# Cross-attention of a Perceiver layer: four of seventeen value steps in three f32r passes, head pairs written out, sums spread one step earlier

## The chip, the cores and the metric

One core of a Trainium2 chip runs the whole kernel in one launch. The time is that of the device in microseconds (us), as the median of several executions. The engines are named as in the profile: PE (TensorE), with its weight loads apart as PEld, DVE (VectorE), ACT (ScalarE), POOL (GpSimd) and SP (SyncE, which only issues DMAs here).

## What is computed

A layer on 256 tokens of 1024 features, in float32: a cross-attention of the normalised tokens over 4096 context rows and the tokens themselves (32 heads, 4 key heads, width 128), then a decayed linear attention, then a small mixture of low-rank experts. The change is in the first part:

```python
q = (latents @ Wq).reshape(b, q_len, N_KV_HEADS, N_GROUPS, HEAD_DIM)
k = (hidden_states @ Wk).reshape(b, kv_len, N_KV_HEADS, HEAD_DIM)
v = (hidden_states @ Wv).reshape(b, kv_len, N_KV_HEADS, HEAD_DIM)
scores = jnp.einsum('bqhgd,bkhd->bhgqk', q, k) * scale
attn = jax.nn.softmax(scores.astype(jnp.float32), axis=-1).astype(q.dtype)
out = jnp.einsum('bhgqk,bkhd->bqhgd', attn, v)
return out.reshape(b, q_len, N_HEADS * HEAD_DIM) @ Wo
```

## The kernel before

Most matrix products are made of three passes in float32r, a rounded float32: each operand is split into a high part (rounded) and a low part (the rest), and `three_pass` (L111) adds high x high, high x low and low x high. One product is not: probabilities by values is a plain float32 matmul (L903), which the trace records as two instructions a tile.

Stages, one after another: `project_keys_values` (stage 1, 0 to 380 us) reads the context in 8 chunks of 512 rows and makes keys (split, kept in DRAM as kT_hi, kT_lo) and values (plain, v_scratch), while POOL splits the query weights. `cross_attention` (380 to 1370 us) runs the 16 pairs of heads. `project_out` (the wo stage) multiplies with Wo, adds x and normalises; `linear_attention`, a second `project_out` and `lora_mixture` follow.

A pair has 17 steps j of 256 key rows, 512 query columns wide (two heads by 256 tokens). The work of two pairs n and n+1 is interleaved, and each engine's order is written out by hand in its slot function; semaphores tie them. In step j:

- PE (`pe_slot`, L925): values of pair n, step j (2 tiles, L903); scores of pair n+1, step j+2 (2 tiles, three passes, L870). After step 5 the predecessor's sums are spread over the partitions (`pe_sums`, L907); after step 15 comes the transpose of the peaks; at the end the maximum is spread and the query projection of pair n+3 is made (48 passes). Two score buffers: scores j+2 wait for ACT's row copy of step j.
- DVE (`dve_slot`, L810): subtracts the maximum from the rows of pair n, step j+1 (`dve_shift`, L790), takes the running peak of pair n+1, step j (`dve_peak`, L765 to L778), and in steps 6 to 9 a quarter each of the reciprocal of the sums (`dve_inverse`, L798).
- ACT (`act_slot`, L661): exp of pair n, step j+1, into one of three buffers `probs` (L649); copy of the score rows of pair n+1, step j (L631); in step 1 also the high part of the predecessor's sums (`act_sum`, L653).
- POOL (`pool_slot`, L726): adds the probabilities of step j to `sums` (L702, L705); in step 3 the low part of the predecessor's sum (`pool_sum_low`, L717), in step 11 the predecessor's output product (L724), at the end the sum of the two halves (L712).
- SP (`sync_slot`, L584): weights of pair n+3, keys of the next key head in every fourth pair, values in the next, by four pieces of columns.

`slots` (L551) runs pair 0, then a hardware loop of three rounds with four pairs each (1 to 12), then pairs 13 to 15 written out. The last pair has no successor: DVE takes four of the sixteen adds there, and PE makes the spread of the sums from plain float32 tiles (`pe_sums_last`, L915).

Of the kernel before, what the change touches and what calls it, by code (L numbers as in the profile page):

```python
# [87 lines left out]
class Shared:  # L88
# [3 lines left out]
    def __init__(self, a):  # L92
# [7 lines left out]
        self.v_stored = a.sem("v_stored")  # L100
        self.first_in = a.sem("first_in")
# [102 lines left out]
def project_keys_values(nc, x, ctxT, wk, wv, wq, x_sb, hT_hi, hT_lo, ident, ones, k_drams, v_dram, wq_drams, shared):  # L204
# [5 lines left out]
    with ExitStack() as ctx:  # L210
        a = Alloc(nc, ctx, "kv_")
        w_raw = a.sb("w_raw", [P, KT, KVH * D])
# [9 lines left out]
        v_out = carve(shared.stage, 0, KVH, CCHUNK // P, D)  # L222
        k_ps = a.ps("k_ps", [P, KVH, BANK])
# [44 lines left out]

        @block.sync
        def _(sp):  # L270
# [12 lines left out]
            with sp.Fori(0, NCHUNK - 3) as c:  # L283
                sp.wait_ge(c_lo_ready, c + 1)
                load(sp, c + 2)
                store(sp, c, VT)
            sp.wait_ge(c_lo_ready, NCHUNK - 2)
            load(sp, NCHUNK - 1)
            store(sp, NCHUNK - 3, VT)
            store(sp, NCHUNK - 2, VT)  # L290
# [8 lines left out]
            store(sp, NCHUNK - 1, VT)  # L299
            store(sp, NCHUNK, QT)  # L300
# [60 lines left out]

        def copy_low_keys(dve, c, n):
# [12 lines left out]
        def _(dve):  # L375
# [92 lines left out]
KEEP = 3  # L468
# [12 lines left out]
def cross_attention(nc, wq_drams, k_drams, v_dram, hT_hi, hT_lo, ident, ones, oT_dram, shared, proj, last_pair):  # L481
# [9 lines left out]
    with ExitStack() as ctx:  # L491
        a = Alloc(nc, ctx, "xa_")
        kT_hi, kT_lo = shared.r
        v = a.sb("v", [P, KV])
        more_rows = a.sb("rows", [P, J - ENDS[0], 2, W])
        rows = [carve(shared.f, 2 * W * j, 2, W) for j in range(ENDS[0])] + [more_rows[:, j] for j in range(J - ENDS[0])]
        probs = [carve(shared.stage, 2 * W * i, 2, W) for i in range(2)] + [a.sb("probs", [P, 2, W])[:, :, :]]
# [24 lines left out]
        v_in = [a.sem(f"v_in{i}") for i in range(len(ENDS))]  # L522
        q_done = a.sem("q_done")
# [25 lines left out]
        def slots(eng, slot):  # L549
# [4 lines left out]
            with eng.Fori(0, KVH - 1) as g:  # L554
# [1262 lines left out]
```

## Time and profile before

| | |
|---|---|
| time, median of 3 runs | 2001.52 us (2000.62 to 2008.04) |
| the profiled execution's own time | 1999.74 us |
| its span | 1997.9 us |
| PE busy | 1960.9 us (98%), granted clock 0.996 of full speed |
| PEld, DVE, ACT, POOL busy | 76%, 62%, 48%, 42% |
| values, plain float32 (L903) | 1088 instructions, 512 us |
| DMA | 283.85 MB, mean 142 GB/s |

A busy matmul is one whose modelled end has not come, so 98% does not say that PE is at its peak; what a tile costs is read from the distance of starts. The chain at the page's end covers only the last 15 us. For the cross-attention the timelines of single engines tell the order, and a releaser in brackets tells what an engine waited for.

### The profile page before, as it was taken

What the parts mean: (1) busy time and instruction counts of PE and PEld (TensorE: products, weight loads), DVE (VectorE), ACT (ScalarE), POOL (GpSimd) and SP (SyncE); (2) the same over time, 40 slices, a digit from 0 to 9 for tenths busy, and PEclk for the clock granted to TensorE, in tenths of its full rate; (3) what the DMA queues carried; (4) which work ended last, traced back from release to release, by engine and by line L of the source; (5) the groups of instructions that cost most, each with busy time, mean ns of one, the idle gap of its engine ahead of it and who ended that gap; (6) DMA issues with size and microseconds to landing.
All of it is one profiled execution on the core that took longest, in us unless ns stands there. A gap on an engine that the chain in (4) does not pass through costs nothing. (4 is left out here: it accounts for less than half of the span.)

```text
span 1997.9 us, 26905 instructions
## 1 busy us (share of the span) xinstructions
PE 1960.9 (98%) x9725; PEld 1516.6 (76%) x9725; DVE 1233.5 (62%) x1294; ACT 952.7 (48%) x1015; POOL 839.3 (42%) x410
## 2 busy tenths in 40 slices
PE   9999999999999999999999999998999999999998
PEld 7888888866666666666666666545899999999876
DVE  4432221266777777877677877787756666666556
ACT  3211110155665565665665665654635444555442
POOL 2545441026776666766767766783000000000200
PEclk9999999999999999999999999999999999999999
DMA  8788875420032210321112210014735544445462
GB/s 306 301 305 318 327 271 190 173 99 25 24 111 90 72 49 15 111 97 56 49 52 92 79 61 1 6 58 180 282 138 189 185 177 175 178 182 189 139 232 99
DMA packets 72224, 283.85 MB, mean 142 GB/s; under 512 B 6400, under 2 KB 24320, under 8 KB 56512
## 3 DMA queue, kind: packets, MB, share of 16 engines
q1 hardware_dynamic: 65216, 232.31, 32.3%
q0 software_dynamic: 6912, 50.33, 6.6%
q8 instruction: 51, 0.84, 0.2%
q14 instruction: 45, 0.37, 0.1%
HBM read 212.89 MB, written 69.73 MB: 141 GB/s over the span
## 5 line engine op out<-in xcount | busy, mean ns | idle before, releaser
L705 POOL TENSOR_TENSOR xa_sums<-xa_sums,stage 128x1024 f32<-128x1024 f32 x150 | 362.7, 2418 | 39.3 <-ACT stage L649 33.1
L903 PE MATMUL xa_o_ps<-stage,xa_v 128*128 128x512 f32 x768 | 361.8, 594 | 4.5 <-ACT stage L649 4.5
L769 DVE TENSOR_TENSOR xa_peak<-xa_s_ps,xa_peak 128x1024 f32<-128x1024 f32 x224 | 273.0, 1219 | 71.4 <-PE xa_s_ps L115 70.8
L113 PE MATMUL xa_s_ps<-xa_qT_hi,split 128*128 128x512 f32 x544 | 304.7, 560 | 6.2 <-issue 3.5
L631 ACT ACTIVATE xa_rows<-xa_s_ps 128x1024 f32<-128x1024 f32 x208 | 213.6, 1027 | 102.0 <-DVE xa_peak L769 69.9
L790 DVE TENSOR_TENSOR xa_rows<-xa_rows,xa_r_ps 128x1024 f32<-128x1024 f32 x208 | 248.1, 1195 | 0.0
L903 PEld LDWEIGHTS xa_o_ps<-stage,xa_v 128*128 128x128 f32 x768 | 144.2, 190 | 116.9 <-issue 99.2
L705 POOL TENSOR_TENSOR xa_sums<-xa_sums,xa_probs 128x1024 f32<-128x1024 f32 x75 | 178.9, 2386 | 124.7 <-ACT xa_probs L649 122.1
L115 PE MATMUL xa_s_ps<-xa_qT_hi,split 128*128 128x512 f32 x544 | 214.4, 394 | 0.0
L114 PE MATMUL xa_s_ps<-xa_qT_lo,split 128*128 128x512 f32 x544 | 212.6, 391 | 0.0
L649 ACT ACTIVATE stage<-xa_rows 128x1024 f32<-128x1024 f32 x144 | 152.5, 1060 | 66.5 <-DVE xa_rows L790 61.6
L1418 DVE TENSOR_TENSOR pair_lo<-pair_raw,pair_hi 128x4096 fp32r<-128x4096 f32 x30 | 132.8, 4426 | 81.4 <-ACT pair_hi L1355 81.4
L1345 POOL TENSOR_TENSOR square_sum<-square_sum,la_squares 128x512 f32<-128x512 f32 x16 | 20.8, 1301 | 385.7 <-ACT la_squares L1385 385.7
L113 PEld LDWEIGHTS xa_s_ps<-xa_qT_hi,split 128*128 128x128 f32 x544 | 102.4, 188 | 78.3 <-issue 41.5
L903 PE MATMUL xa_o_ps<-xa_probs,xa_v 128*128 128x512 f32 x320 | 150.5, 593 | 1.7 <-ACT xa_probs L649 1.7
L114 PEld LDWEIGHTS xa_s_ps<-xa_qT_lo,split 128*128 128x128 f32 x544 | 102.7, 189 | 65.1 <-issue 52.0
L113 PE MATMUL la_qk_ps<-hT_hi,pair_hi 128*128 128x256 f32 x512 | 145.6, 284 | 0.3 <-PEq L1018 0.3
L115 PE MATMUL la_qk_ps<-hT_hi,pair_lo 128*128 128x256 f32 x512 | 144.8, 283 | 0.0
L114 PE MATMUL la_qk_ps<-hT_lo,pair_hi 128*128 128x256 f32 x512 | 144.7, 283 | 0.0
L307 ACT ACTIVATE kv_k_hi<-kv_k_ps 128x512 fp32r<-128x512 f32 (+1 forms) x36 | 20.4, 573 | 209.0 <-DMA kT_lo_scratch<-kv_k_lo 105.4
L115 PEld LDWEIGHTS xa_s_ps<-xa_qT_hi,split 128*128 128x128 f32 x544 | 102.0, 188 | 23.6
L366 DVE TENSOR_TENSOR kv_k_lo<-kv_k_ps,kv_k_hi 128x512 fp32r<-128x512 f32 (+1 forms) x36 | 23.6, 659 | 138.4 <-ACT kv_k_hi L307 138.4
(308 smaller groups left out, 4629.7 us busy)
## 6 DMA issues: line engine op xcount, KB each, us to landing
pair_raw<-in_w_qk SPq DMA_DIRECT2D x15, 2048.0 KB, 7.7
pair_raw<-in_w_gv SPq DMA_DIRECT2D x15, 2048.0 KB, 7.7
kv_w_raw<-in_wq POOLq DMA_DIRECT2D x16, 1024.0 KB, 8.3
wq_hi_scratch<-x_hT_hi POOLq DMA_DIRECT2D x16, 1024.0 KB, 4.5
wq_lo_scratch<-x_hT_lo POOLq DMA_DIRECT2D x16, 1024.0 KB, 5.3
full<-in_wo SPq DMA_DIRECT2D x16, 1024.0 KB, 5.1
pair_raw<-in_w_out SPq DMA_DIRECT2D x16, 1024.0 KB, 5.0
xa_w_hi<-wq_hi_scratch SPq DMA_DIRECT2D x15, 1024.0 KB, 4.8
```

The costliest lines, as they stand in the source:

```text
L113: pe.matmul(out, w_hi, m_hi, start=first, stop=False)
L114: pe.matmul(out, w_hi, m_lo, start=False, stop=False)
L115: return pe.matmul(out, w_lo, m_hi, start=False, stop=last)
L366: dve.tensor_tensor(k_lo[:, g % 2, 0:n], k_ps[:, g, 0:n], f32(k_hi[:, g % 2, 0:n]), ALU.subtract).then_inc(k_copied, 1)
L631: act.activation(rows[j], s_ps[:, 2 * b:2 * b + 2, :], ACT.Copy).then_inc(row_ready, 1)
L649: act.activation(probs[j % KEEP], rows[j], ACT.Exp, scale=SCALE).then_inc(exp_done, 1)
L705: pool.tensor_tensor(sums[:, :, :], sums[:, :, :], probs[j % KEEP], ALU.add).then_inc(added, 1)
L769: dve.tensor_tensor(peak[:, :, :], s_ps[:, 2 * b:2 * b + 2, :], peak[:, :, :], ALU.max).then_inc(peak_done, 1)
L790: dve.tensor_tensor(rows[j], rows[j], r_ps[:, :].unsqueeze(1).to_broadcast([P, 2, W]), ALU.subtract).then_inc(shifted, 1)
L903: last = pe.matmul(o_ps[:, :], v[:, at], probs[j % KEEP][:, t, :], start=j == 0 and t == 0, stop=j == J - 1 and t == 1)
L1345: pool.tensor_tensor(square_sum[:, :, :], square_sum[:, :, :], squares[:, :, :], ALU.add).then_inc(sq_added, 1)
L1418: dve.tensor_tensor(w_lo[part][:, :, :], raw[part][:, :, :], f32(w_hi[part][:, :, :]), ALU.subtract).then_inc(w_lo_ready[part], 1)
```

## The change

- In steps 2, 6, 10 and 14 of each pair the value product is made in three f32r passes. Stage 1 splits the values of those tiles (`split_values` on DVE) and stores the low parts in a tensor of their own; a pair loads v, v_hi and v_lo. ACT makes the exp of such a step twice, once into `probs` and once rounded into `probs_hi`; POOL subtracts (`pool_low`) into `probs_lo`. There is one tile each of probs_hi and probs_lo. The row sums still take the unrounded `probs`.
- `probs` has four buffers (KEEP) in place of three, and shift and exp run two steps ahead (AHEAD) in place of one.
- The loop over key heads is written out in every engine's program.
- The sum's high part moves from ACT's step 1 to step 0, its low part from POOL's step 3 to step 1, the spread on PE from step 5 to step 4, the reciprocals from steps 6 to 9 to 5 to 8.
- To make room, `inverse` shares the tile of `sum_row`, x is a tile of stage 1 and loaded a second time in the wo stage, and the identity and the ones are rounded once, in the first block, and no longer in the attention's.

```diff
 LAST_BY_POOL = tuple(j for j in range(1, J) if j not in LAST_BY_VECTOR)
-KEEP = 3
+SPLIT_STEPS = (2, 6, 10, 14)
+SPLIT = len(SPLIT_STEPS)
+KEEP = 4
+AHEAD = 2
...
-            with eng.Fori(0, KVH - 1) as g:
+            for g in range(KVH - 1):
                 for u in (1, 2, 3, 0):
                     slot(eng, 4 * g + (u or 4), u, g if u else g + 1)
...
         def act_exp(act, n, j, first=False, last=False):
...
             act.activation(probs[j % KEEP], rows[j], ACT.Exp, scale=SCALE).then_inc(exp_done, 1)
+            if j in SPLIT_STEPS:
+                i = SPLIT_STEPS.index(j)
+                if i > 0:
+                    act.wait_ge(pv_done, J * n + SPLIT_STEPS[i - 1] + 1)
+                elif not first:
+                    act.wait_ge(pv_done, J * (n - 1) + SPLIT_STEPS[-1] + 1)
+                act.activation(probs_hi[:, :, :], rows[j], ACT.Exp, scale=SCALE).then_inc(probs_hi_ready, 1)
...
-                if has_prev and j == 1:
+                if has_prev and j == 0:
                     act_sum(act, n - 1)
...
+        def pool_low(pool, n, j):
+
+            pool.wait_ge(exp_done, J * n + j + 1)
+            pool.wait_ge(probs_hi_ready, SPLIT * n + SPLIT_STEPS.index(j) + 1)
+            pool.tensor_tensor(probs_lo[:, :, :], probs[j % KEEP], f32(probs_hi[:, :, :]), ALU.subtract).then_inc(low_by_pool, 1)
...
-                if has_prev and j == 3:
+                if j in SPLIT_STEPS:
+                    pool_low(pool, n, j)
+                if has_prev and j == 1:
                     pool_sum_low(pool, n - 1)
...
-                if has_prev and 6 <= j < 10:
-                    dve_inverse(dve, n - 1, j - 6)
+                if has_prev and 5 <= j < 9:
+                    dve_inverse(dve, n - 1, j - 5)
...
+            if j in SPLIT_STEPS:
+                pe.wait_ge(low_by_pool, SPLIT * n + SPLIT_STEPS.index(j) + 1)
+                for t in range(2):
+                    at = slice(split_columns(j).start + t * P, split_columns(j).start + (t + 1) * P)
+                    last = three_pass(pe, o_ps[:, :], v_hi[:, at], v_lo[:, at], probs_hi[:, t, :], probs_lo[:, t, :],
+                                      False, False)
+                last.then_inc(pv_done, 1)
+                return
...
-                if has_prev and j == 5:
+                if has_prev and j == 4:
                     pe_sums(pe, n - 1)
```

In stage 1 and in the wo stage:

```diff
+        def split_values(dve, c, t, i):
+
+            dve.wait_ge(v_ready, VT * c + t + 1)
+            dve.tensor_copy(v_out[:, :, t, :].bitcast(F32R), v_ps[:, t, :].rearrange("p (g d) -> p g d", d=D)).then_inc(v_rounded, 1)
+            dve.wait_ge(v_rounded, 2 * i + t + 1)
...
+                    last = dve.tensor_tensor(tile, v_ps[:, t, g0 * D:g1 * D].rearrange("p (g d) -> p g d", d=D),
+                                             v_out[:, g0:g1, t, :], ALU.subtract).then_inc(low_copied, 1)
...
+            if i == 3:
+                sp.dma_start(x_sb[:, :, :], x).then_inc(x_in, 16)
             weights.load_half(sp, i // 2, i % 2)
```

How the hand-written orders move shows at two places. The first is POOL's program from the end of pair 0 into pair 1. `xa_sum_row` is the predecessor's sum, `xa_sum_hi` its high part from ACT, `xa_exp_done` and the like are semaphores. Before:

```order
L702 TENSOR_TENSOR xa_sums<-stage 128x1024 [waits xa_sum_made,xa_exp_done]
...
L705 TENSOR_TENSOR xa_sums<-xa_sums,xa_probs 128x1024 [waits xa_added]
...
L705 TENSOR_TENSOR xa_sums<-xa_sums,stage 128x1024 [waits xa_added]
L717 TENSOR_TENSOR xa_sum_lo<-xa_sum_row,xa_sum_hi 128x512 [waits xa_sum_made,xa_sum_hi_ready]
```

and now:

```order
L814 TENSOR_TENSOR xa_sum_row<-xa_sums 128x512 [waits xa_added]
L798 TENSOR_TENSOR xa_sums<-stage 128x1024 [waits xa_sum_made,xa_exp_done]
L819 TENSOR_TENSOR xa_sum_lo<-xa_sum_row,xa_sum_hi 128x512 [waits xa_sum_made,xa_sum_hi_ready]
L801 TENSOR_TENSOR xa_sums<-xa_sums,xa_probs0 128x1024 [waits xa_added,xa_exp_done]
L807 TENSOR_TENSOR xa_probs_lo<-xa_probs0,xa_probs_hi 128x1024 [waits xa_probs_hi_ready,xa_exp_done]
L801 TENSOR_TENSOR xa_sums<-xa_sums,xa_probs1 128x1024 [waits xa_added,xa_exp_done]
```

The sum's low part stands behind the first add (step 1) in place of the third (step 3), ahead of the first probs_lo. The second place is ACT's program at a split step (step 10 of pair 0, whose exp is issued in step 8), now:

```order
L718 ACTIVATE xa_rows<-xa_s_ps 128x1024 [waits xa_exp_done,xa_peak_done]
L736 ACTIVATE xa_probs0<-xa_rows 128x1024 [waits xa_added,xa_pv_done,xa_shifted]
L743 ACTIVATE xa_probs_hi<-xa_rows 128x1024 [waits xa_pv_done]
L718 ACTIVATE xa_rows<-xa_s_ps 128x1024 [waits xa_exp_done,xa_peak_done]
L736 ACTIVATE xa_probs1<-xa_rows 128x1024 [waits xa_added,xa_pv_done,xa_shifted]
```

Two exps stand between two row copies there, where one stood before.

## Rows read from the trace of the kernel before

**Rows 1.** Timeline of ACT, 660 to 800 us: start, us, engine, line, operation, [idle <- releaser]
```profile
668.30 0.60 ACT L659 ACTIVATE xa_o_raw<-xa_o_ps 128x512 f32<-128x512 f32 x1 [1.48 <-PE xa_o_ps L903]
...
728.20 0.60 ACT L659 ACTIVATE xa_o_raw<-xa_o_ps 128x512 f32<-128x512 f32 x1 [1.48 <-PE xa_o_ps L903]
...
790.13 0.60 ACT L659 ACTIVATE xa_o_raw<-xa_o_ps 128x512 f32<-128x512 f32 x1 [1.48 <-PE xa_o_ps L903]
```

**Rows 2.** Timeline of PE where the loop turns round
```profile
736.13 0.49 PE L113 MATMUL xa_s_ps<-xa_qT_hi,split 128*128 128x512 f32 x1 [1.79 <-issue]
```

**Rows 3.** Timeline of PE, pair 13 (x4: two f32 tiles)
```profile
1220.06 1.88 PE L903 MATMUL xa_o_ps<-stage,xa_v 128*128 128x512 f32 x4
1221.38 0.79 PE L113 MATMUL xa_s_ps<-xa_qT_hi,split 128*128 128x512 f32 x1
...
1223.17 1.88 PE L903 MATMUL xa_o_ps<-stage,xa_v 128*128 128x512 f32 x4
...
1238.67 0.40 PE L912 MATMUL xa_t_ps<-xa_sum_hi,xa_ones_r 128*128 128x512 f32 x1
...
1239.13 1.88 PE L903 MATMUL xa_o_ps<-stage,xa_v 128*128 128x512 f32 x4
```

**Rows 4.** Timeline of POOL, pair 13
```profile
1216.02 2.41 POOL L702 TENSOR_TENSOR xa_sums<-stage 128x1024 f32<-128x1024 f32 x1 [6.37 <-ACT stage L649]
...
1224.99 2.40 POOL L705 TENSOR_TENSOR xa_sums<-xa_sums,stage 128x1024 f32<-128x1024 f32 x1 [0.17 <-ACT stage L649]
1227.34 1.30 POOL L717 TENSOR_TENSOR xa_sum_lo<-xa_sum_row,xa_sum_hi 128x512 fp32r<-128x512 f32 x1
1228.59 2.39 POOL L705 TENSOR_TENSOR xa_sums<-xa_sums,stage 128x1024 f32<-128x1024 f32 x1
1231.12 2.39 POOL L705 TENSOR_TENSOR xa_sums<-xa_sums,xa_probs 128x1024 f32<-128x1024 f32 x1
```

**Rows 5.** Timeline of ACT, pair 13
```profile
1213.83 2.11 ACT L649 ACTIVATE stage<-full 128x1024 f32<-128x1024 f32 x2 [1.90 <-DVE full L790]
1220.16 1.02 ACT L631 ACTIVATE full<-xa_s_ps 128x1024 f32<-128x1024 f32 x1 [4.22 <-DVE xa_peak L765]
...
1222.42 1.03 ACT L631 ACTIVATE full<-xa_s_ps 128x1024 f32<-128x1024 f32 x1
1223.35 0.62 ACT L653 ACTIVATE xa_sum_hi<-xa_sum_row 128x512 fp32r<-128x512 f32 x1
...
1244.47 1.06 ACT L649 ACTIVATE stage<-xa_rows 128x1024 f32<-128x1024 f32 x1 [0.92 <-DVE xa_rows L790]
1245.60 1.02 ACT L631 ACTIVATE xa_rows<-xa_s_ps 128x1024 f32<-128x1024 f32 x1
```

**Rows 6.** Timeline of DVE, pair 13
```profile
1218.90 1.22 DVE L765 COPY xa_peak<-xa_s_ps 128x1024 f32<-128x1024 f32 x1 [4.05 <-PE xa_s_ps L115]
...
1239.33 0.96 DVE L798 RECIPROCAL xa_inverse<-xa_t_ps 128x128 f32<-128x128 f32 x1 [2.34 <-PE xa_t_ps L913]
1240.20 1.16 DVE L790 TENSOR_TENSOR xa_rows<-xa_rows,xa_r_ps 128x1024 f32<-128x1024 f32 x1
...
1242.41 0.95 DVE L798 RECIPROCAL xa_inverse<-xa_t_ps 128x128 f32<-128x128 f32 x1
```

**Rows 7.** Timeline of PE, start of pair 14
```profile
1276.24 0.50 PE L113 MATMUL xa_s_ps<-xa_qT_hi,split 128*128 128x512 f32 x1 [0.18 <-ACT full L631]
```

**Rows 8.** Timeline of POOL, pair 15, first and last add
```profile
1329.69 2.37 POOL L735 TENSOR_TENSOR xa_sums<-stage 128x1024 f32<-128x1024 f32 x1 [5.38 <-ACT stage L649]
...
1363.19 3.14 POOL L738 TENSOR_TENSOR xa_sums<-xa_sums,stage 128x1024 f32<-128x1024 f32 x1
```

**Rows 9.** Timeline of POOL, rounding of the constants
```profile
382.44 0.28 POOL L748 CAST xa_ident_r<-ident 128x128 fp32r<-128x128 f32 x1 [74.92 <-POOLq L210]
```

**Rows 10.** Busy time by stretch: us, PE, PEld, DVE, ACT, POOL, clock, DMA share, GB/s
```profile
150.00:200.00 50.00, 50.00 (x222) 41.41 (x221) 12.39 (x10) 6.63 (x6) 25.24 (x16) 1.00 0.84 317
1375.00:1450.00 75.00, 75.00 (x332) 62.10 (x331) 54.49 (x55) 42.97 (x50) 0.00 (x0) 1.00 0.80 292
```

More of the change, by code:

```diff
@@ L282, in _ @@
             sp.dma_start(x_sb[:, :, :], x).then_inc(x_in, 16)
[L283 to L286, printed above, removed]
+            sp.wait_ge(c_lo_ready, 1)
+            load(sp, 2)
+            store(sp, 0, VT)
+            with sp.Fori(0, (NCHUNK - 4) // 2) as i:
+                for par in range(2):
+                    c = 2 * i + 1 + par
+                    sp.wait_ge(c_lo_ready, c + 1)
+                    load(sp, c + 2)
+                    store(sp, c, VT)
+                    if par == 0:
+                        store_low(sp, c, i)
             sp.wait_ge(c_lo_ready, NCHUNK - 2)
@@ L478, in starts_piece, with plain_columns, split_columns, value_runs @@
     return j == 0 or j in ENDS
-def cross_attention(nc, wq_drams, k_drams, v_dram, hT_hi, hT_lo, ident, ones, oT_dram, shared, proj, last_pair):
+def plain_columns(j0, j1):
+    back = sum(s < j0 for s in SPLIT_STEPS)
+    return slice(2 * P * (j0 - back), 2 * P * (j1 - back))
+def split_columns(j):
+    i = SPLIT_STEPS.index(j)
+    return slice(2 * P * i, 2 * P * (i + 1))
+def value_runs(i):
+    runs, start = [], ENDS[i - 1] if i else 0
+    for j in range(start, ENDS[i]):
+        if j in SPLIT_STEPS:
+            if start < j:
+                runs.append((start, j))
+            runs.append((j, j + 1))
+            start = j + 1
+    if start < ENDS[i]:
+        runs.append((start, ENDS[i]))
+    return runs
+def cross_attention(nc, wq_drams, k_drams, v_dram, low_dram, hT_hi, hT_lo, ident, ident_r, ones_r, oT_dram, shared, proj, last_pair):
     with ExitStack() as ctx:
@@ L677, in act_slot @@
                 act_output(act, n, not has_prev)
-                act_exp(act, n + 1, 0)
+                for j in range(AHEAD):
+                    act_exp(act, n + 1, j, last=last and u == 2)
         @block.scalar
@@ L686, in _ @@
                     act_query(act, 1, 1)
-            act_exp(act, 0, 0, True)
+            for j in range(AHEAD):
+                act_exp(act, 0, j, True)
             slots(act, act_slot)
@@ L839, in _ @@
             dve_max(dve, 0, True)
-            dve_shift(dve, 0, 0)
+            for j in range(AHEAD):
+                dve_shift(dve, 0, j)
             slots(dve, dve_slot)
@@ L921, in pe_sums_last @@
             for i, part in enumerate(pieces):
-                last = pe.matmul(t_ps[:, :], ones[:, :], part, start=i == 0, stop=i == len(pieces) - 1)
+                last = pe.matmul(t_ps[:, :], f32(ones_r[:, :]), part, start=i == 0, stop=i == len(pieces) - 1)
             last.then_inc(sum_spread, 1)
```

124 lines of the change are left out of this document (87 added, 37 removed).

## The prediction, made before the changed kernel ran

> **What bounds the kernel now.** I read the page first: PE 98% busy, POOL 42%, and a chain that names only the last microseconds. So the views that matter are those of one stage. The cross-attention (430 to 1370 us) runs as 16 nearly equal head pairs; [rows 1] gives the moments at which ACT copies a pair's output: 59.90 us from one pair to the next, and 61.93 where the loop turns round, with a hole of 1.79 us in PE's stream [rows 2]. Elsewhere PE issues without a gap inside a pair, so the pair's length is PE's, and whatever PE newly waits for lands in the time.
>
> [rows 3] is PE in pair 13, which is straight-line code already, as all pairs will be. I call V0 = 1220.06 the start of value step 0. Scores of the next pair start at V0 + 1.31, and V1 is at V0 + 3.11: a step is 3.10 us. One f32r pass is 0.23 us (1238.67 to 1239.13 are two), so a step's six score passes take 1.38 and its two f32 tiles 1.72.
>
> [rows 4] is POOL. An add of the row sums runs 2.39 us; a dependent add follows after 2.53 (1228.59 to 1231.12), an independent instruction after 2.35 (1224.99 to 1227.34), and behind the half-size subtraction the next starts after 1.25. [rows 5] is ACT: an exp and its successor are 1.13 apart, a score-row copy and the next 0.93; POOL starts 0.08 after ACT's end. [rows 6] is DVE: it idles 4.05 us before the first peak copy, and in the four steps with a reciprocal its cycle is 3.08 us (1239.33 to 1242.41), the shift 0.87 behind the reciprocal. That is PE's step almost exactly: in these steps PE has no lead.
>
> **Part 1, the gain on PE.** 4 of 17 steps a pair go from 1.72 us of f32 to six f32r passes, 6 x 0.23 = 1.38: 0.34 less a step, 1.36 a pair. The last pair is not PE's (below), so 15 x 1.36 = 20.4 us is what is offered. Bounds: 0.31 to 0.38 a step, as the passes next to f32 work are slower or not. The Trainium skill, "FP8 and Floating Point Precision", section "TensorE Precision Notes", has true FP32 as four passes through the array; three in place of four would give back a quarter of 1.72, 0.43 a step, and the offered gain would be 25.8, the sum below 5.4 less. I take the row, since a pass with its weight load measures 0.23, not 1.72/8 = 0.215.
>
> **Part 2, the loop.** The loop over key heads turns round twice, and the pair there is 61.93 - 59.90 = 2.03 longer. Written out, both go: -4.1. The entry and the exit of the loop cost nothing that the periods show.
>
> **Part 3, POOL gets 4 subtractions a pair and an earlier wait.** Each split step's values wait for probs_lo, which POOL makes behind its add of the same step. Total work is no problem: 16 adds, 4 subtractions and three half-size ones are some 53 us of 60. The order is. POOL's program has, in a pair with a predecessor: add 1, then the low part of the predecessor's sum, then add 2, then probs_lo of step 2. The sum's low part waits for its high part, which ACT makes behind the row copy of the next pair's step 0; that copy starts at V0 + 0.10 [rows 5], because it needs the peak copy and this the scores. So, with V0 = 0: ACT sum_hi at 0.10 + 0.93 = 1.03, end 1.65; POOL sum_lo at 1.73 (it idles from the end of add 1, -1.63, to here), add 2 at 2.98, probs_lo at 5.33, end 7.73. PE wants it at 3.11 + 3.10 = 6.21 and gets it at 7.78: **a stall of 1.57 us**. Before, the same wait stood behind add 3 and cost nothing.
>
> Behind this POOL runs on: a block of four steps is 3 x 2.53 + 2 x 2.35 = 12.29 for POOL and 3 x 3.10 + 2.76 = 12.06 for PE. probs_lo of step 6 ends at 20.0, wanted at 20.3; of step 10 at 32.3; of step 14, with the output product (1.25) in between, at 45.7.
>
> **Part 4, ACT and DVE in the reciprocal steps.** The sums are spread after step 4 now, one step earlier for PE and DVE alike, V5 = 17.20. From there DVE's chain runs by the cycle of [rows 6]: shift 9 at V5 + 0.20 + 3.08 + 0.87 = 4.15, and ACT's exp 1.19 behind its start (1244.47 against 1243.28), the row copy 1.13 later, 1.02 long, then PE's scores after 0.06: V5 + 7.55. PE, one cheaper step in hand (step 6), wants them at 3.10 + 2.76 + 1.31 = 7.17. The next is worse: step 10's second exp (probs_hi, 1.13) stands ahead of row copy 8, so the scores start at 7.22 + 1.19 + 1.13 + 1.13 + 1.02 + 0.06 = 11.75 where PE without stalls is there at 10.27: **1.48 us lost**. What PE saved in step 6 is thus given back, and the exp on top. V14 comes out at 45.9, just behind POOL's 45.7, so that step 14 costs nothing more; if Part 4 were nil, POOL would hold PE at 45.7 anyway. The pair is longer by 1.57 + 1.48 - 1.36 = **+1.7 us**. From V16 to the next V0 nothing changes: exps of the next pair need POOL's add 16, at about 48.2, in time.
>
> The sum over pairs. Pair 0 has no predecessor, hence neither wait: -1.4. Pairs 1 to 13: 13 x 1.7 = +22.1. Pair 14 follows without a query projection between; ACT has exp 2 and its second copy (2 x 1.13) before row copy 0, on which PE already waits there [rows 7]: 1.7 + 2.3 = +4.0. Pair 15 has no next one, and POOL sets its end: 36.6 us from its first add to its last [rows 8], of which 12 adds at 2.53 and two products at 1.25 are 32.9. Four more instructions of 2.35 are 9.4; if they filled all the slack of 3.7 it would be +5.7, if new waits (for sum_hi, for the single probs_hi tile, free only after PE's split step) arise, up to +10. I take +8, nearer the upper end because each subtraction there sits between an exp and a PE step that frees the next.
>
> **Part 5, the rest.** The constants are now rounded in the first block, before anything else may start: two casts of 0.28 [rows 9], +0.6. Stage 1's extra copies and subtractions on DVE (4 chunks, 2 tiles each, some 0.7 us apiece) and 2 MB of stores on SP's queue lie beside a PE that has not one idle slice [rows 10] and a value bank that is needed a chunk later; cost 0, and if DMA at 0.84 of its share should choke, about 3 us. The value loads go from 4 to more, smaller transfers a group, wanted a pair later: 0. x is loaded a second time (1 MB) in the output projection, ahead of the last quarter weights; at 292 GB/s [rows 10] that is 3.4 us of DMA with 0.2 of the share free: 0 taken, 3 as the bound.
>
> Sum: 0.6 - 1.4 + 22.1 + 4.0 + 8.0 - 4.1 = **+29.2 us** on the profiled execution's own 1999.74, so 2028.9. The median of the runs shown is 1.8 above it: **2031 us**, slower by 1.5%.
>
> **The rivals.**
> *It does what it is written for* (10%). PE is the bound and stays it; the waits of Parts 3 and 4 are absorbed. For it: POOL has 42% on the page and 53 of 60 us now. Against it: PE has no slack in a pair, and the wait for sum_hi has no earlier work behind it that could hide. Then -15 x 1.36 - 4.1 + 8 + 0.6 = -16: 1985.
> *Only ACT's chain bites, POOL is in time at step 2* (8%), say because the high part of the sum comes earlier than I have it. A pair is then +1.48 - 1.36 = +0.1, and pair 14 +2.4: 13 x 0.1 + 2.4 + 8 - 1.4 - 4.1 + 0.6 = +7: 2006 to 2010, no change or just slower.
> *Only POOL bites* (inside my forecast): a pair is +1.4 by the 45.7 above, 2027.
> *More is queued than I see* (7%): POOL stretches when DVE works in SBUF alone, the x load holds up the projection, PE's clock falls in the new pauses. 15 x 1 us more and 3 for x: 2045 to 2050. The decision between same and slower is at one place, the start of probs_lo of step 2: if it started before V0 + 3.7 no pair would stall there.
>
> **How the numbers follow.** Forecast with its bounds 75%: 2015 (pairs at 1.0, the last at 5.7) to 2040. The range that leaves out no more than 2 in 10 takes in the upper part of the ACT-only case: 2010 to 2042. About 0.5% (10 us) is what a measurement of this kernel can tell from no change. Slower by more than that: the forecast and the bad case, 0.82, and a little of ACT-only, 0.83. Within it: 0.07. Faster: 0.10.
>
> **What would show it.** Right: pair period about 61.5 us without a longer one at the loop's old ends; in POOL's waits an entry of the sum's low part on ACT's sum_hi of some 3.4 us, 14 times; PE waiting 1.6 us on POOL's probs_lo at step 2, and on ACT's row copies about 1.5 us a pair at steps 7 and 8; the last pair 8 us longer. Wrong: a period under 59, or PE waiting nowhere inside a pair; a period over 63 would say that a queue is longer than I have it.

## The result and the profile after

The changed kernel takes **2034.74 us**, median of 4 runs (2032.27 to 2036.05), the kernel before on the same chip 2002.07 us (2000.62 to 2008.04). The ratio is 1.0156, with a 95% interval of 1.0141 to 1.0172: slower by 1.6%, 3.7 us above the forecast of 2031 and inside its range. The profiled execution took 2034.6 us. Its page begins:

```profile
span 2032.8 us, 26010 instructions
## 1 busy us (share of the span) xinstructions
PE 1958.4 (96%) x9853; PEld 1540.3 (76%) x9853; DVE 1266.1 (62%) x1306; ACT 1007.7 (50%) x1079; POOL 990.5 (49%) x474
```

PE is still busy for 96%, and POOL for 49% only. By these shares nothing but PE could be the bound, and they mislead here. What answers to [rows 1], ACT's copy of a pair's output, in the timeline of ACT after the change:

```profile
672.05 0.60 ACT L753 ACTIVATE xa_o_raw<-xa_o_ps 128x512 f32<-128x512 f32 x1 [1.41 <-PE xa_o_ps L1016]
733.47 0.60 ACT L753 ACTIVATE xa_o_raw<-xa_o_ps 128x512 f32<-128x512 f32 x1 [1.41 <-PE xa_o_ps L1016]
794.86 0.60 ACT L753 ACTIVATE xa_o_raw<-xa_o_ps 128x512 f32<-128x512 f32 x1 [1.41 <-PE xa_o_ps L1016]
```

61.42 and 61.39 us apart; from pair 0 to pair 13 (487.91 to 1285.96) the mean is 61.39, and no pair is longer where the loop turned round. Where PE stopped inside pair 13 (V0 = 1233.32), all its gaps from V0 to V14 in the timeline of PE, and V8 and V9 around the second:

```profile
1241.07 0.50 PE L114 MATMUL xa_o_ps<-xa_probs_hi,xa_v_hi 128*128 128x512 f32 x1 [1.38 <-POOL xa_probs_lo L807]
...
1259.67 1.88 PE L1016 MATMUL xa_o_ps<-stage,xa_v 128*128 128x512 f32 x4
...
1261.98 0.50 PE L114 MATMUL xa_s_ps<-xa_qT_hi,split 128*128 128x512 f32 x1 [0.44 <-ACT xa_rows L718]
...
1263.47 1.88 PE L1016 MATMUL xa_o_ps<-stage,xa_v 128*128 128x512 f32 x4
...
1279.02 0.50 PE L114 MATMUL xa_o_ps<-xa_probs_hi,xa_v_hi 128*128 128x512 f32 x1 [0.23 <-POOL xa_probs_lo L807]
```

V2 starts at V0 + 7.75, the scores of tile 10 at V5 + 11.38, V14 at V0 + 45.70. A bracket counts from the modelled end of the matmul before and is shorter than what the step loses. The distance of starts tells the loss: V1 to V2 is 4.64 us in place of 3.10 (1.54 lost), V8 to V9 3.80 in place of 3.11 (0.69), V13 to V14 3.49 in place of 3.10 (0.39).

POOL in the same pair, against [rows 4]:

```profile
1235.04 1.30 POOL L819 TENSOR_TENSOR xa_sum_lo<-xa_sum_row,xa_sum_hi 128x512 fp32r<-128x512 f32 x1 [3.35 <-ACT xa_sum_hi L747]
1236.29 2.39 POOL L801 TENSOR_TENSOR xa_sums<-xa_sums,xa_probs 128x1024 f32<-128x1024 f32 x1
1238.63 2.38 POOL L807 TENSOR_TENSOR xa_probs_lo<-xa_probs,xa_probs_hi 128x1024 fp32r<-128x1024 f32 x1
...
1276.57 2.40 POOL L807 TENSOR_TENSOR xa_probs_lo<-xa_probs,xa_probs_hi 128x1024 fp32r<-128x1024 f32 x1
1278.90 2.88 POOL L801 TENSOR_TENSOR xa_sums<-xa_sums,xa_probs 128x1024 f32<-128x1024 f32 x1
```

From the end of the first of these rows to the last one POOL waits for nothing. So the idle column of its last low half is empty, although PE waits for it. The view of the waits, whole span (us in total, times, the longest):

```profile
PEld xa_o_ps L114 <- POOL xa_probs_lo L807: 53.3, 33, 7.2
POOL xa_sum_lo L819 <- ACT xa_sum_hi L747: 44.9, 15, 3.4
PE xa_o_ps L114 <- POOL xa_probs_lo L807: 38.1, 31, 6.4
```

In the last pair, PE's gaps at the split steps, and then POOL's first and last add against [rows 8]:

```profile
1357.38 0.79 PE L114 MATMUL xa_o_ps<-xa_probs_hi,xa_v_hi 128*128 128x512 f32 x1 [6.39 <-POOL xa_probs_lo L807]
1379.09 0.80 PE L114 MATMUL xa_o_ps<-xa_probs_hi,xa_v_hi 128*128 128x512 f32 x1 [4.95 <-POOL xa_probs_lo L807]
1391.76 0.79 PE L114 MATMUL xa_o_ps<-xa_probs_hi,xa_v_hi 128*128 128x512 f32 x1 [3.53 <-POOL xa_probs_lo L807]
```

```profile
1348.39 2.37 POOL L837 TENSOR_TENSOR xa_sums<-stage 128x1024 f32<-128x1024 f32 x1 [4.32 <-ACT stage L736]
...
1391.67 2.82 POOL L840 TENSOR_TENSOR xa_sums<-xa_sums,xa_probs 128x1024 f32<-128x1024 f32 x1
```

The difference of the two spans is 34.9 us. It adds up as follows; a pair is taken from one output copy to the next, the last one from the last copy to the first product of the output projection:

| stretch | forecast | measured |
|---|---|---|
| up to the first V0 | +0.6 | +0.4 |
| pair 0 | -1.4 | -1.2 |
| pairs 1 to 13, with the loop's -4.1 | +18.0 | +15.5 |
| pair 14 (54.53, now 58.44) | +4.0 | +3.9 |
| pair 15 (45.34, now 59.64) | +8.0 | +14.3 |
| projection and the rest | 0 | +1.9 |

The first and the last row are no measure of the change. In the executions of kernels that are alike up to there V0 lies between 436.97 and 441.63, and the old kernel with only its loop written out took 3.3 us more than the kernel before behind the cross-attention, where their code is the same.

### The profile page after: what moved, and what is told of

It reads as the page before. It is cut to its first block and busy times, and to the rows that moved or that the text cites. A ratio compares the mean times of both kernels' runs of the same rounds, so it can differ in the third digit from the quotient of the medians.

```text
span 2032.8 us, 26010 instructions
## 1 busy us (share of the span) xinstructions
PE 1958.4 (96%) x9853; PEld 1540.3 (76%) x9853; DVE 1266.1 (62%) x1306; ACT 1007.7 (50%) x1079; POOL 990.5 (49%) x474
## 5 line engine op out<-in xcount | busy, mean ns | idle before, releaser
L801 POOL TENSOR_TENSOR xa_sums<-xa_sums,xa_probs 128x1024 f32<-128x1024 f32 x120 | 294.9, 2457 | 6.6
L114 PE MATMUL xa_s_ps<-xa_qT_hi,split 128*128 128x512 f32 x544 | 274.8, 505 | 10.5 <-ACT xa_rows L718 6.3
L1016 PE MATMUL xa_o_ps<-stage,xa_v 128*128 128x512 f32 x576 | 270.1, 592 | 2.6 <-ACT stage L736 2.6
L801 POOL TENSOR_TENSOR xa_sums<-xa_sums,stage 128x1024 f32<-128x1024 f32 x105 | 250.0, 2381 | 13.0
L116 PE MATMUL xa_s_ps<-xa_qT_hi,split 128*128 128x512 f32 x544 | 214.0, 393 | 0.0
L1016 PEld LDWEIGHTS xa_o_ps<-stage,xa_v 128*128 128x128 f32 x576 | 107.8, 189 | 86.1 <-issue 76.4
L114 PEld LDWEIGHTS xa_s_ps<-xa_qT_hi,split 128*128 128x128 f32 x544 | 102.3, 188 | 83.9 <-issue 30.8
L807 POOL TENSOR_TENSOR xa_probs_lo<-xa_probs,xa_probs_hi 128x1024 fp32r<-128x1024 f32 x64 | 153.8, 2403 | 0.0
L736 ACT ACTIVATE stage<-xa_rows 128x1024 f32<-128x1024 f32 x112 | 118.4, 1059 | 69.2 <-DVE xa_rows L892 63.7
L798 POOL TENSOR_TENSOR xa_sums<-stage 128x1024 f32<-128x1024 f32 x15 | 36.1, 2406 | 195.9 <-ACT stage L736 195.9
L1016 PE MATMUL xa_o_ps<-xa_probs,xa_v 128*128 128x512 f32 x256 | 124.5, 610 | 0.0
```

Source lines behind the costliest of these rows:

```text
L114: pe.matmul(out, w_hi, m_hi, start=first, stop=False)
L116: return pe.matmul(out, w_lo, m_hi, start=False, stop=last)
L736: act.activation(probs[j % KEEP], rows[j], ACT.Exp, scale=SCALE).then_inc(exp_done, 1)
L798: pool.tensor_tensor(sums[:, :, :], probs[0], probs[1], ALU.add).then_inc(added, 1)
L801: pool.tensor_tensor(sums[:, :, :], sums[:, :, :], probs[j % KEEP], ALU.add).then_inc(added, 1)
L807: pool.tensor_tensor(probs_lo[:, :, :], probs[j % KEEP], f32(probs_hi[:, :, :]), ALU.subtract).then_inc(low_by_pool, 1)
```

## The experiments

Each kernel was timed beside the kernel before on the same chip, but not all on one chip; so they are compared with each other by the ratio. The period is the mean from pair 0's output copy to pair 13's, the last pair as above, both from the profiled execution.

| kernel | us | ratio to before (95%) | period | last pair |
|---|---|---|---|---|
| before, loop written out | 1997.4 | 0.9967 (0.9953 to 0.9980) | 59.81 | 45.34 |
| the change | 2034.7 | 1.0156 (1.0141 to 1.0172) | 61.39 | 59.64 |
| sum's low half at step 3 | 2006.0 | 1.0013 (1.0004 to 1.0023) | 59.20 | 56.64 |
| ACT's second exp behind the row | 2039.6 | 1.0185 (1.0168 to 1.0202) | 61.85 | 59.39 |
| the same, small maximum | 2034.4 | 1.0161 (1.0140 to 1.0182) | 61.38 | 59.25 |
| both moves | 2002.4 | 0.9994 (0.9984 to 1.0004) | 59.00 | 56.60 |
| low half ahead of the add | 2001.6 | 0.9988 (0.9976 to 1.0000) | 59.22 | 55.61 |
| last pair's low halves on DVE | 2024.0 | 1.0111 (1.0094 to 1.0128) | 61.39 | 47.13 |
| no low halves | 1989.8 | 0.9946 (0.9929 to 0.9962) | 59.20 | 44.25 |
| four moves | 1989.5 | 0.9936 (0.9915 to 0.9956) | 58.76 | 48.61 |
| four moves, product at 14 | 1982.3 | 0.9913 (0.9884 to 0.9942) | 58.51 | 48.63 |

### The sum's low half back at step 3

```diff
-                if has_prev and j == 1:
+                if has_prev and j == 3:
                     pool_sum_low(pool, n - 1)
```

> The changed kernel with one step moved: POOL's subtraction for the low half of the sum stands at step 3 again, behind that step's add, in place of ahead of step 2's add. Everything else of the change stays. Theory (POOL's queue): POOL no longer waits 3.4 us for ACT's sum_hi ahead of probs_lo of step 2, so the stall of TensorE on it (1.38 us in pair 13) and the small one at step 14 (0.23 us and the adds behind it) go in pairs 1 to 14: some 1.5 to 1.9 us a pair, the period goes from 61.4 to 59.5 to 59.9 us, and the last pair starts its adds earlier. Time 2034.7 less 21 to 30: 2005 to 2014 us, 2009 taken. Rival (the sum of POOL's work is the bound, wherever the subtraction stands): the wait comes back in front of another low half, time 2030 to 2035 us. Second rival (ScalarE's second exponential is the whole of it): the wait on POOL goes but the period stays within 0.3 us of 61.4.

Measured: 2006.0 us, the period 2.19 us shorter. That is 0.3 us more than I expected of the period; the time is inside the range. POOL's timeline shows the wait gone, and the low half starts at V0 + 0.85 in place of V0 + 5.31, 4.5 us earlier; PE's only gap from V0 (1210.14) to V14 is on a row copy:

```profile
1208.65 2.40 POOL L801 TENSOR_TENSOR xa_sums<-xa_sums,xa_probs 128x1024 f32<-128x1024 f32 x1
1210.99 2.41 POOL L807 TENSOR_TENSOR xa_probs_lo<-xa_probs,xa_probs_hi 128x1024 fp32r<-128x1024 f32 x1
1213.35 2.39 POOL L801 TENSOR_TENSOR xa_sums<-xa_sums,xa_probs 128x1024 f32<-128x1024 f32 x1
1215.70 1.30 POOL L819 TENSOR_TENSOR xa_sum_lo<-xa_sum_row,xa_sum_hi 128x512 fp32r<-128x512 f32 x1
```

```profile
1237.13 0.50 PE L114 MATMUL xa_s_ps<-xa_qT_hi,split 128*128 128x512 f32 x1 [0.41 <-ACT xa_rows L718]
```

One moved line of POOL's program carries 28.7 of the 32.7 us by which the medians of before and the change differ. The rival by which POOL's total work is the bound falls: the work is the same. So does the one that puts all of it on ACT's second exponential, which is still where it was.

### ACT's second exponential behind the row copy

```diff
+                if j == 0:
+                    act_hi(act, n, AHEAD, not has_prev)
                 if has_next:
                     act_row(act, n + 1, (u + 1 + j) % 2, j)
+                if 0 < j < J - AHEAD:
+                    act_hi(act, n, j + AHEAD, not has_prev)
```

(`act_hi` is the second activation with its two waits, taken out of `act_exp`.)

> The changed kernel with one move on ScalarE: the second exponential of a split tile (its rounded high half) stands behind the row copy of its step, in place of between the first exponential and the row copy, so that the scores of the next pair are not held by it. Theory: TensorE's waits on the row copies in the steps of the reciprocals get shorter by some 0.9 us for a split step (the exponential's pitch is 0.94 to 0.97 us), but POOL's queue still holds step 2 and the low half of step 14, which keep the distance from V2 to V14; so little of it reaches the end: 0 to 0.5 us a pair, 2027 to 2035 us. Rival (ScalarE alone sets the period): the whole 1.0 to 1.4 us a pair comes back, 2013 to 2020 us.

Measured: 2039.6 us, a period of 61.85, **longer** by 0.46. Both theories missed the sign. The timelines of PE, POOL and DVE at step 14 of one pair (V0 = 1175.72):

```profile
1221.88 0.50 PE L114 MATMUL xa_o_ps<-xa_probs_hi,xa_v_hi 128*128 128x512 f32 x1 [1.43 <-POOL xa_probs_lo L813]
```

```profile
1216.68 2.38 POOL L807 TENSOR_TENSOR xa_sums<-xa_sums,xa_probs 128x1024 f32<-128x1024 f32 x1
1219.02 2.81 POOL L813 TENSOR_TENSOR xa_probs_lo<-xa_probs,xa_probs_hi 128x1024 fp32r<-128x1024 f32 x1
```

```profile
1218.65 0.95 DVE L880 TENSOR_TENSOR xa_peak<-xa_peak 128x512 f32<-128x512 f32 x1
```

PE is ready for V14 at 1221.88 - 1.43 = V0 + 44.73, 0.7 us earlier than after the change (V0 + 45.70 - 0.23). So the second exponential did delay PE, and taking it away brought nothing: POOL's queue holds V14 in both. That queue is now 0.4 us longer, because the last low half takes 2.81 us in place of 2.40. Beside it stands DVE's maximum of the two halves of `peak`. The changed kernel has it too, but there it starts under the last low half (1276.57 above) and the instruction that gets longer is the add behind, 2.88 us, for which PE does not wait:

```profile
1276.98 2.53 DVE L874 TENSOR_TENSOR xa_peak<-xa_peak 128x512 f32<-128x512 f32 x1
```

PE's earlier scores have moved it in front of the low half.

### The same with a maximum of one column

```diff
-                    dve.tensor_tensor(peak[:, 0, :], peak[:, 0, :], peak[:, 1, :], ALU.max)
+                    dve.tensor_tensor(peak[:, 0, 0:1], peak[:, 0, 0:1], peak[:, 1, 0:1], ALU.max)
```

> The kernel with ScalarE's second exponential behind the row copy (the one that came out slower than the changed kernel), and DVE's one maximum that reads and writes SBUF alone (behind the peak of step 13) cut from 512 columns to one: the shift of a row is so taken without the second half of the first fourteen tiles. Theory (POOL's queue sets where V14 stands, and there the maximum, which TensorE's earlier scores had moved in front of POOL's last low half, stretches it from 2.38 to 2.81 us): without it the low half takes 2.4 us again, and the period goes from 61.85 back to 61.39 us or a little under: 2039.6 less 14 by 0.46, 2033 us (2030 to 2035). Rival (the second exponential, now later, delays the low half itself, and DVE has no part in it): the period stays at 61.8 to 61.9 us, 2039 us.

The edit leaves out the maximum over the other 511 columns. Measured: 2034.4 us, a period of 61.38, as expected. POOL, DVE, and PE at V14 of the next pair (V0 = 1233.63):

```profile
1215.51 2.39 POOL L813 TENSOR_TENSOR xa_probs_lo<-xa_probs,xa_probs_hi 128x1024 fp32r<-128x1024 f32 x1
```

```profile
1215.14 0.43 DVE L880 TENSOR_TENSOR xa_peak<-xa_peak 128x1 f32<-128x1 f32 x1
```

```profile
1279.32 0.50 PE L114 MATMUL xa_o_ps<-xa_probs_hi,xa_v_hi 128*128 128x512 f32 x1 [0.93 <-POOL xa_probs_lo L813]
```

The whole 0.46 us a pair were DVE's maximum in front of POOL's low half. V14 is back at V0 + 45.69, where the changed kernel has it. PE comes there 0.7 us earlier and waits 0.7 us longer: with POOL as it is, ACT's second exponential has no price at all.

### Both moves together

This is the edit of the first experiment and that of the second.

> Both single moves together: POOL's low half of the sum at step 3, ScalarE's second exponential behind the row copy. Theory (two separate queues, each with its own price): neither POOL nor ScalarE holds TensorE, the gain of the split tiles themselves (1.36 us a pair) is left, and the period is 58.5 to 59.0 us against 61.4: 14.5 pairs by 2.4 to 2.9 us, 1992 to 2000 us, 1996 taken. Rival (one cause only): no more than the better of the single moves, 2005 to 2014 us. Rival (the split tiles give no gain on TensorE at all): a period of 59.9 us, 2009 to 2013 us.

Measured: 2002.4 us and a period of 59.00, 0.20 below the first move alone: outside the range I gave. The period is at the upper edge of what I expected, and the last pair gave 3.0 us only. Neither rival holds either. PE still has one gap in a pair (here at V0 + 43.3), and it is POOL's again:

```profile
1250.87 0.50 PE L114 MATMUL xa_o_ps<-xa_probs_hi,xa_v_hi 128*128 128x512 f32 x1 [0.24 <-POOL xa_probs_lo L813]
```

What ACT gave back ran into the next limit of POOL's queue.

### Low halves ahead of their add

```diff
             for j in range(1, J):
+                if j in SPLIT_STEPS:
+                    pool_low(pool, n, j)
                 if has_next:
                     pool_add(pool, n, j, not has_prev)
...
-                if j in SPLIT_STEPS:
-                    pool_low(pool, n, j)
```

> The changed kernel with one exchange on POOL: in a split step the subtraction that makes the low half stands ahead of that step's add, in place of behind it; the sum's low half stays where the change put it, so POOL still waits some 3.4 us for sum_hi. Theory (POOL's queue from probs_lo of step 2 to probs_lo of step 14 sets the pair, 45.6 us of it in the changed kernel): each low half is there one add, 2.4 us, earlier, both stalls of TensorE go (1.38 us at step 2, 0.24 us and more at step 14), the period falls from 61.39 us to 59.0 to 59.3 us, as it did when the subtraction was moved back, and the time to 2034.7 less 14 by 2.2 and 1 to 6 us of the last pair: 1997 to 2004 us, 2001 taken. Rival (the place of the subtraction for the sum is the cause, whatever order the rest has): the period stays above 60.5 us, 2018 us or more. Second rival (the adds come too late for the probability buffers, and ScalarE waits): 2010 to 2030 us, with waits of ScalarE's exponentials on POOL's adds.

Measured: 2001.6 us and a period of 59.22, both as expected. The view of the waits still has `POOL xa_sum_lo <- ACT xa_sum_hi` with 44.9 us, 15 times, exactly as in the changed kernel. The wait that looked like the culprit is all there and costs nothing in the period, since what stands between it and the low half was shortened by one add.

### The last pair's low halves on DVE

```diff
-                if j in SPLIT_STEPS:
+                if j in SPLIT_STEPS and has_next:
                     pool_low(pool, n, j)
...
+                if not has_next and j in SPLIT_STEPS:
+                    pool_low(dve, n, j)
```

> The changed kernel with the four low halves of the last pair alone made by DVE, in place of POOL; the other pairs are as they were. Theory (in the last pair POOL's adds and low halves together, 46.1 us against 36.6 us before, are the chain that ends it, and TensorE's waits of 6.4, 5.0 and 3.5 us let its clock fall): POOL's queue there is back at 36 to 38 us, the three waits and the stretches at a mean granted clock under 0.8 go, and the last pair takes 46 to 50 us against 59.6: 2022 to 2026 us, 2023 taken; the period of the other pairs stays at 61.4 us. Rival (DVE is as full, or is stretched beside POOL where both work in SBUF, as its 2.5 us maximum was): 2028 to 2033 us. Rival (the last pair's loss is the clock alone, whatever the engine): 2033 to 2036 us.

Measured: 2024.0 us; the last pair 47.13, 12.5 us shorter, as expected. PE still waits there for DVE's low halves, at most 2.61 and 3.12 us, and the clock granted to TensorE still dips (0.68 from 1364 to 1368 us). POOL's first add and its last two:

```profile
1348.33 2.37 POOL L837 TENSOR_TENSOR xa_sums<-stage 128x1024 f32<-128x1024 f32 x1 [4.33 <-ACT stage L736]
...
1380.29 6.47 POOL L840 TENSOR_TENSOR xa_sums<-xa_sums,xa_probs 128x1024 f32<-128x1024 f32 x2
```

38.4 us from the first to the end of the last, against 46.1 with the low halves on POOL. From POOL's end to the projection's first product it is 4.7 us here and in the kernel before; it was 9.5 in the changed one. There V16 and the spread of the sums stand like this in PE's timeline:

```profile
1397.79 1.88 PE L1016 MATMUL xa_o_ps<-stage,xa_v 128*128 128x512 f32 x4
1399.50 1.88 PE L1035 MATMUL xa_t_ps<-xa_sums,ones 128*128 128x512 f32 x4
```

Busy time by stretch just ahead of the projection, the changed kernel and then this one (PEclk is the third column from the right):

```profile
core 0: us, PE busy (x) PEld busy (x) DVE busy (x) ACT busy (x) POOL busy (x), PEclk, DMA share, GB/s
1392.00:1400.00 8.00, 8.00 (x16) 4.26 (x17) 4.70 (x3) 0.30 (x1) 2.48 (x1) 0.65 0.00 0
```

```profile
1384.00:1391.00 7.00, 6.24 (x14) 2.22 (x13) 5.58 (x4) 1.03 (x2) 2.76 (x1) 1.00 0.00 0
```

### No low halves

```diff
-                if j in SPLIT_STEPS:
-                    pool_low(pool, n, j)
...
-                pe.wait_ge(low_by_pool, SPLIT * n + SPLIT_STEPS.index(j) + 1)
+                pe.wait_ge(probs_hi_ready, SPLIT * n + SPLIT_STEPS.index(j) + 1)
...
-                    last = three_pass(..., probs_hi[:, t, :], probs_lo[:, t, :],
+                    last = three_pass(..., probs_hi[:, t, :], probs_hi[:, t, :],
```

> The changed kernel without any low half of the probabilities: POOL does not subtract, and TensorE's second pass takes the high half in its place, at the same shapes; the kernel's low product of the split tiles is so left out. Theory: with POOL out of the way what is left in pairs 1 to 14 is TensorE's own gain (1.36 us a pair) less what ScalarE's second exponential costs. A period of 59.2 us (as with the subtraction moved back) says that exponential costs 0.7 us a pair; 58.5 us says it costs nothing and the rest was POOL too; over 59.5 us (my forecast's 1.48 us a pair) says it was ScalarE after all. The last pair within 3 us of the kernel before, 45 to 49 us. Time 1990 to 2001 us, 1994 taken. Rival (TensorE gains nothing with the three passes): a period of 59.8 us or more, 2001 us or more.

Measured: 1989.8 us and a period of 59.20, as with the subtraction moved back. The time is 0.2 us and the last pair (44.25) 0.8 us below what I expected. ACT's output copies and PE's one gap between them:

```profile
1196.73 0.60 ACT L753 ACTIVATE xa_o_raw<-xa_o_ps 128x512 f32<-128x512 f32 x1 [1.41 <-PE xa_o_ps L1014]
...
1255.92 0.60 ACT L753 ACTIVATE xa_o_raw<-xa_o_ps 128x512 f32<-128x512 f32 x1 [1.41 <-PE xa_o_ps L1014]
```

```profile
1232.47 0.50 PE L114 MATMUL xa_s_ps<-xa_qT_hi,split 128*128 128x512 f32 x1 [0.44 <-ACT xa_rows L718]
```

With the sum's low half at step 3, POOL's low halves cost nothing in the period: it is 59.20 with them and without them. What is left is ACT's: V8 to V9 is 3.8 us here and 3.1 in the two versions below, which have the second exponential behind the row copy.

### The loop alone, and the combinations

```diff
-            with eng.Fori(0, KVH - 1) as g:
+            for g in range(KVH - 1):
```

> The kernel before with only its loop over groups of four pairs written out. Theory: the two turns of the loop cost 2.0 us each (the pair at a turn has 61.9 us against 59.9), so it is 4.1 us faster: 1998 us (1997 to 1999). Rival: the turn's cost is given back by the fetch of four times the instructions, or is no cost of the loop at all: 2001 to 2003 us.

Measured: 1997.4 us, the last pair unchanged; the expected 4.1 us lie at the edge of the interval (ratio 0.9953 to 0.9980, 4 to 9 us). By the trace pairs 1 to 13 are 4.9 us shorter: 4.1 at the two turns, and the other eleven pairs have 59.81 us in place of 59.88. This is what a version of the split must beat.

> The changed kernel with four moves together: the sum's low half at step 3, ScalarE's second exponential behind the row copy, POOL's low halves ahead of the add of their step, and the last pair's low halves on DVE. Theory: the two single moves of the queues left 59.00 us a pair, with a last stall of 0.24 us on the low half of step 14 and TensorE's own work at 58.5 us; the exchange on POOL takes that stall: 58.4 to 58.8 us. With the last pair at 46 to 50 us: 2002.4 less 14 by 0.4 less 7 to 11: 1986 to 1991 us, 1988 taken, faster than both kernels. Rival (the rest of 0.5 us a pair is not POOL's but in TensorE's own order, as in the steps of the row copies): a period of 58.9 to 59.0 us and 1992 to 1995 us.

Measured: 1989.5 us. The period came to 58.76 and the last pair to 48.61, both inside what was expected, with a rest of a stall at step 14 (PEld's own pace is 0.24). First PEld, then POOL:

```profile
1187.21 0.19 PEld L114 LDWEIGHTS xa_o_ps<-xa_probs_hi,xa_v_hi 128*128 128x128 f32 x1 [0.44 <-POOL xa_probs_lo L813]
```

```profile
1178.64 1.28 POOL L832 TENSOR_TENSOR head_out<-xa_o_raw,xa_sum_row 128x512 f32<-128x512 f32 x1
1179.88 4.94 POOL L807 TENSOR_TENSOR xa_sums<-xa_sums,stage 128x1024 f32<-128x1024 f32 x2
1184.76 2.40 POOL L813 TENSOR_TENSOR xa_probs_lo<-xa_probs,xa_probs_hi 128x1024 fp32r<-128x1024 f32 x1
```

So the product `head_out`, which nobody waits for at that moment, was moved behind:

```diff
-                if has_prev and j == 11:
+                if has_prev and j == (14 if has_next else 11):
                     pool_output(pool, n - 1, 1 - u % 2, 8 * (n - u % 2) + 16)
```

> The version with the four moves, and in it POOL's product of the predecessor's output (half size, 1.25 us) at step 14 in place of step 11, except in the last pair. Theory: POOL's queue up to the low half of step 14 still holds TensorE by 0.20 us a pair (the wait on it is 0.44 us where 0.24 is the engine's own pace); with 1.25 us less ahead of it that goes: a period of 58.5 to 58.6 us against 58.76, 2 to 3 us of the time, 1985 to 1988 us. Rival (the wait moves to the row copies, or the product at step 14 makes the copy of the output wait): 58.76 us or more, 1989 us or more.

Measured: **1982.3 us**, better than expected by more than the period explains: in the profiled executions 13 x 0.25 = 3.3 us come from the period, 1.9 from pair 14 (56.96, now 55.09) and 2.8 from the time ahead of the first V0 (439.78, here 436.97). The last of these is no merit of the edit, which changes nothing up to there: the clock granted to TensorE was 1.00 from 425 to 435 us here, and 0.73 and then 0.59 in the version with the four moves. Why pair 14 is shorter was not looked into. ACT's output copies:

```profile
1188.28 0.60 ACT L755 ACTIVATE xa_o_raw<-xa_o_ps 128x512 f32<-128x512 f32 x1 [1.41 <-PE xa_o_ps L1024]
...
1246.80 0.60 ACT L755 ACTIVATE xa_o_raw<-xa_o_ps 128x512 f32<-128x512 f32 x1 [1.41 <-PE xa_o_ps L1024]
```

Its interval (0.9884 to 0.9942) lies below that of the loop alone (0.9953 to 0.9980): with its queues in order the split in three passes pays on top of the loop, by 11 us if the ratios are taken, and by 15 if the medians are, which come from different chips.

## Why the prediction was right, and where it was not

**Part 1, PE's gain: right.** With the queues out of the way the period is 58.51 against 59.81 written out: 1.30 us a pair, forecast 1.36. In the last version the steps from V2, V10 and V14 are 2.74 to 2.75 us in place of 3.10, and the one from V6 is 2.87. The Trainium skill, "FP8 and Floating Point Precision", section "TensorE Precision Notes", counts four passes for true FP32, so that three would save a quarter of the 1.72 us, an estimate of 1.7 a pair. The measured 1.30 decides for the row's 0.34 a step.

**Part 2, the loop: right.** No pair is longer at its old ends, and alone it gives 4.1 us at the turns and 0.8 more in the other pairs.

**Part 3, POOL: right.** V2 at V0 + 7.75 (forecast 7.78), the wait for sum_hi 3.35 us in each of pairs 1 to 13 (some 3.4, 14 times) and 1.14 and 0.23 in the last two, V14 at 45.70 (45.7). The experiment with the subtraction at step 3 takes the stall away. The one with the low half first takes it away too and leaves the wait as it is: the wait costs only with that add between it and the low half.

**Part 4, ACT: the place right, the size not, and the addition wrong.** I had 1.48 us for the row copy behind the second exponential; by the distance of V8 and V9 it costs 0.69. Three things make the difference. I had given an exponential 1.13 us to whatever follows; behind an exponential the next one starts after 0.97 and the row copy after 0.94, so the scores of tile 10 came at V5 + 11.38, not 11.75. PE's step 6 saves 0.26 us only, so PE is there at 10.38, not 10.27. And I took the start of a score that waited from one that did not: in the rows the first score pass behind f32 tiles starts 0.64 us ahead of the second, behind a wait 0.34, so 0.30 of the late start is no loss.

By the distance of starts PE would have been ready for V14 at 45.3, not 45.9. Then POOL's 45.7 decides. My sentence that POOL would hold PE at 45.7 if Part 4 were nil was the right account, and "+1.57 + 1.48 - 1.36" was the wrong one: the prices of two queues that meet at one instruction do not add, the later one sets it. The runs show this from both sides. With the exponential behind the row copy and DVE's maximum out of the way, nothing is won (61.39 and 61.38). Without POOL's delay 2.19 are won, more than the 1.57 I had for it. Only when POOL is out of the way does the exponential have a price of its own, 59.20 to 58.51 = 0.7 us a pair.

That the sum of a pair came out near is in part luck, since two errors stand against each other: the exponential 0.8 us too large, and at step 14 nothing for POOL, which holds PE there by 0.39. Another 0.1 comes at each of the two waits on POOL, because the first pass behind a wait takes 0.34 us. "Only POOL bites" (+1.4 a pair, priced at 2027) and the forecast's sum (+1.7) differ by 0.3 us a pair. Against the old kernel written out the pair is longer by 1.58 (61.39 and 59.81), between the two; what decides for the first is the experiments, not the size.

**The last pair: the mechanism right, the term mis-sized**, +14.3 for +8. I had counted POOL's queue only: it grew from 36.6 to 46.1 us, 9.5, inside my bound of 10. The other 4.8 us are behind POOL's end, 9.5 us in place of 4.7. Before, PE had its last value step behind it (end 1364.8) when POOL ended its last add (1366.3). Now PE starts V14 only after the last low half (1391.76) and ends V16 when its spread of the sums starts (1399.50), 5.0 us behind POOL's end at 1394.49. V14 and V15 run at the lower level of 1.2 GHz: the granted clock is 0.53 from 1391.8 to 1398 us. By the steps of the other pairs V14 to V16 take 4.9 us at full clock, 1.5 + 1.7 + 1.7, and here they take 7.7. So, as an estimate from these rows, some 2.8 of the 4.8 us are the clock and 2 the later work. With the low halves on DVE both parts go, 12.5 of the 14.3 us; what stays is POOL's queue, 38.4 us for 36.6.

**Part 5: small, and not resolved.** The 0.4 us up to the first V0 lie inside the spread of 4.7 us that executions have there, so they don't show what the constants cost (0.6 forecast). The projection stage is 0.8 us longer (96.92 against 96.12). It has 96.7 to 97.7 us in all versions with the split and 96.35 in the old kernel written out, so something there seems to cost 0.3 us or more; that it is x's second load was not tried. The other 1.1 us are within what kernels with the same code show. No run took the fourth buffer or the second step ahead (KEEP, AHEAD) back, so what these give by themselves is open.

The errors partly cancel: pairs 1 to 13 came 2.5 us shorter than the sum, the last pair 6.3 and the rest 1.9 longer. By the profiled execution the forecast was 5.7 us short, by the median 3.7; the latter is the nearer one only because the profiled execution of the kernel before was 2.3 us below its median and that of the changed kernel 0.1.

## What to carry to other kernels

An engine that is half idle can set the pace, if between two things that the bound engine waits for its queue has no gap: lay its instructions end to end from the one to the other and compare with the bound engine's own way. Where two queues meet the bound engine at one instruction, take the later, not the sum; removing the one that is not last brings nothing. In a queue, put first what is waited for at once, and move what nobody waits for (here a product and the sum's low half) behind it. With the last pair's low halves on DVE, four such moves turned 2034.7 us into 1982.3.

## What was not expected of the hardware

- **DVE's maximum and POOL's instructions shut each other out for whole instructions.** The maximum with two inputs in SBUF (128x512) ends 0.54 to 0.55 us behind the end of the POOL instruction under which it starts, whether that ends 0.4 us after its start (0.95 us long, second exponential behind the row) or 2.0 us after (2.53 to 2.56 us long, changed kernel). POOL's next instruction then takes 2.81 to 2.88 in place of 2.39 us; with one column of maximum it takes 2.39 again. DVE's other maxima, with an input in PSUM, took 1.22 us and stretched nothing. The Trainium skill, "SBUF — State Buffer", section "SBUF: two separate sides", has the shared port pair of these two engines as an exclusive lock that goes to whichever starts first, for the whole instruction, and names a DVE instruction with two SBUF inputs against a POOL one that reads SBUF; by that rule, the trace agrees. The 0.46 us a pair came from a speed-up of PE that moved the maximum onto the instruction for which PE waits.
- **Pitch depends on the pair of instructions.** On ACT a rounded exponential of the same input follows an exponential after 0.97 us and the row copy follows that after 0.94, where exponential to row copy is 1.13.
- **The granted clock fell in the last pair, and ahead of the first V0 in some executions only.** Between, the changed kernel's gaps of 1.4 us a pair leave it at 1.00 (1100 to 1150 us). In its last pair, after gaps of 6.4, 5.0 and 3.5 us, stretches of 4 us stand at 0.50 to 0.56, the level of 1.2 GHz; the kernel before has one there, 0.57 from 1328 to 1332 us, after a gap of 2.56. Ahead of the first V0 all versions have the same code for PE, and two gaps of 1.4 to 1.6 us. From 430 to 435 us the granted clock was then 0.50 in the version with the sum's low half at step 3, 0.59 in the one with the four moves and 1.00 in the last one. Their first V0 are 441.63, 439.78 and 436.97 (1.9 us of the first had come about before 385 us); such a difference says nothing on an edit.
